# Graph attention on one Trainium2 core: edge rows gathered once per chunk of edges instead of once per step, steps addressed through a register

## The reference

```python
def _transformer_conv(x, src, dst, qw, qb, kw, kb, vw, vb, sw, sb):
    q = (x @ qw + qb).reshape(N, H, D); k = (x @ kw + kb).reshape(N, H, D); v = ...
    alpha = jnp.einsum('ehd,ehd->eh', q[dst], k[src]) * scale
    m = jax.ops.segment_max(alpha, dst, num_segments=N)
    ex = jnp.exp(alpha - m[dst])
    denom = jax.ops.segment_sum(ex, dst, num_segments=N)
    w = ex / (denom[dst] + 1e-16)
    agg = jax.ops.segment_sum(w[:, :, None] * v[src], dst, num_segments=N)
    return agg.mean(axis=1) + x @ sw + sb
h = _transformer_conv(x, src, dst, layer 1) + x @ lin1_w + lin1_b
out = _transformer_conv(h, src, dst, layer 2) + h @ lin2_w + lin2_b
return _layernorm(x + out, axis=-1)
```

## Time and profile before

| | |
|---|---|
| time, median of 3 runs | 1239.3 us (1238.72 to 1239.43) |
| profiled execution, span from first to last instruction | 1238.0 us, 30556 instructions |
| PE busy | 993.4 us (80%) |
| DVE busy | 983.5 us (79%) |
| ACT busy | 784.5 us (63%) |
| POOL busy | 801.5 us (65%), 832 gathers |
| mean granted TensorE clock | 0.940 |

### The profile page before, as it was taken

One profiled execution on the slowest core, in us unless ns is written; L12 is line 12 of the kernel. 1 busy time (PEld: TensorE's weight loads), 2 busy tenths in 40 slices (PEclk: granted clock), 3 DMA queues, 4 the chain that ended last, 5 costly groups with the idle time before them and its releaser, 6 DMA issues.

```text
span 1238.0 us, 30556 instructions
## 1 busy us (share of the span) xinstructions
PE 993.4 (80%) x6796; PEld 791.4 (64%) x6796; DVE 983.5 (79%) x5252; ACT 784.5 (63%) x2594; POOL 801.5 (65%) x854
## 2 busy tenths in 40 slices
PE   4868987878877878789896776978886878888887
PEld 2647766766666667678653655757675757667775
DVE  4799986878787878889567687878787887879876
ACT  0456866676676768677254564758575768678655
POOL 3777777777777777750057777777777777777100
PEclk9989999899999999999797999999899999999888
DMA  4223332222222222210032222222232323222001
GB/s 112 88 77 89 89 84 80 78 80 80 78 81 80 78 82 84 73 42 1 27 102 79 79 80 77 80 80 78 80 87 71 89 73 85 77 80 63 17 2 52
DMA packets 53531, 90.21 MB, mean 73 GB/s; under 512 B 17499, under 2 KB 25969, under 8 KB 53361
## 3 DMA queue, kind: packets, MB, share of 16 engines
q0 software_dynamic: 26624, 54.58, 16.4%
q1 hardware_dynamic: 24145, 32.62, 8.7%
q10 hardware_dynamic: 2592, 1.07, 0.3%
HBM read 84.86 MB, written 3.34 MB: 71 GB/s over the span
## 4 chain that ended last, share of the span: by engine, by line
DMA 28%; PE 21%; POOL 20%; issue 15%; DVE 13%; ACT 2%; DVEq 1%; SPq 0%; POOLq 0%; ACTq 0%
POOL gathered L407 20%; DMA gathered<-h_rows,src_e 14%; DMA gathered<-in_x,src_e 14%; PE ps L679 9%; PE ps L667 5%; DVE acc L961 4%; DVE junk L930 3%; PE ps L767 2%; PE ps L751 1%; PE ps L762 1%; ACT whot L508 1%; DVE max_b L999 1%; DVE apart L941 1%; DVE max_f L997 1%; PE ps L655 0%
## 5 line engine op out<-in xcount | busy, mean ns | idle before, releaser
L508 ACT ACTIVATE whot<-apart,below 128x128 f32<-128x128 bf16 x1664 | 550.3, 388 | 139.7 <-DVE apart L941 127.5
L679 PE MATMUL ps<-gathered,whot 128*128 128x129 f32 x3328 | 566.1, 297 | 62.4 <-ACT whot L508 44.0
L930 DVE SCALAR_TENSOR_TENSOR junk<-ps,gathered 128x129 f32<-128x129 f32 x1664 | 413.0, 286 | 163.6 <-issue 113.8
L667 PE MATMUL ps<-table,hot_t 128*128 x2496 | 445.7, 287 | 101.8 <-DVE junk L930 80.5
L679 PEld LDWEIGHTS ps<-gathered,whot 128*128 128x128 f32 x3328 | 457.1, 200 | 100.0 <-DVE acc L961 64.7
L407 POOL DMA_INDIRECT gathered<-in_x,src_e x416 | 399.8, 961 | 144.3 <-issue 68.0
L407 POOL DMA_INDIRECT gathered<-h_rows,src_e x416 | 397.5, 955 | 126.6 <-issue 62.2
L667 PEld LDWEIGHTS ps<-table,hot_t 128*128 128x128 bf16 x2496 | 249.3, 100 | 212.3 <-issue 157.3
L961 DVE TENSOR_TENSOR acc<-ps,acc 128x258 f32 x832 | 350.2, 421 | 14.9 <-PE ps L679 5.4
L492 ACT ACTIVATE apart<-col_b,ndl_e 128x128 bf16<-128x128 bf16 x618 | 239.2, 387 | 0.0
L930 DVE DVE_READ_ACCUMULATOR junk<-ps,gathered 128x1 f32 x1664 | 134.9, 81 | 0.4
(11 more groups left out here) (165 smaller groups left out, 561.0 us busy)
## 6 DMA issues: line engine op xcount, KB each, us to landing
dl_bc<-local_dst_rows SPq DMA_DIRECT2D x104, 256.0 KB
gathered<-in_x,src_e POOLq DMA_INDIRECT x416
gathered<-h_rows,src_e POOLq DMA_INDIRECT x416
h_rows<-table SPq DMA_DIRECT2D x6, 256.0 KB, 2.3
out<-x_rows SPq DMA_DIRECT2D x6, 256.0 KB
table<-in_L_gnn_q_w ACTq DMA_DIRECT2D x2, 128.0 KB
table<-in_L_gnn_k_w ACTq DMA_DIRECT2D x2, 128.0 KB
wv<-in_L_gnn_v_w ACTq DMA_DIRECT2D x2, 128.0 KB
```

What stands on the lines that cost most here:

```text
L508: last = nc.scalar.activation(whot[:, c % UN, h, :], apart[:, c % UN, :], ACT.Exp, scale=FAR, bias=below[:, j % 2, h, o:o + 1])
L667: last = nc.tensor.matmul(bank_t[n % NB][:, 0:CW], hot_t[:, n // BC % 2, t % BC, :], table[:, bass.ds(b, 1), part, :].rearrange("p o c -> ...
L679: last = nc.tensor.matmul(bank_u[n % NB][:, h * C1:(h + 1) * C1], whot[:, c % UN, h, :], gathered[:, c % RING, :], start=True, stop=True)
L930: last = V.scalar_tensor_tensor(out=junk[:, t % 2, h, :], in0=bank_t[n % NB][:, h * C1:(h + 1) * C1], scalar=1.0, in1=gathered[:, t % RING ...
```

## The change

POOL gathers each chunk once: 391 gathers a layer in place of 416, chunk c into slot c % 98. All steps of a chunk read that one slot. As the chunk of a step depends on the data, `step_alpha` on DVE and `step_u` on PE take the slot number from a register, loaded from a new list `slot_i`, and `bins_of` and `slots_of` now load eight steps at a time (RB = 8) where one list was loaded by four. `step_alpha(t)` still waits for gather t, and from step 391 on for none. A slot is free once all bins that its chunk can have are done, which is 24 steps later than before, so gather c waits for u step c - 74 where it waited for c - 98.

The indices no longer need `sel`: `src_e` is the transposed source list, 128 chunks from a first transpose, the rest from three more. SP loads the source list first, DVE converts it first, PE transposes it first, and DVE's other preparation stands behind that. `prepare(1)` has a 97th row for the slots, and a few small DVE instructions compute chunk modulo 98.

```diff
-                bin_i[0:1, step:step + UN], engines=[etype], min_val=0, max_val=BINS - 1,
+                bin_i[0:1, step:step + RB], engines=[etype], min_val=0, max_val=BINS - 1,
+        def slots_of(etype, step):
+            _, v = nc.values_load_multi_w_load_instructions(
+                slot_i[0:1, step:step + RB], engines=[etype], min_val=0, max_val=RING - 1,
...
+        def newest(t):
+            return min(t, CHUNKS - 1)
@@ sync
-            sp.wait_ge(S["pads_set"], 4)
-            for d, t in ((dst_d, dst_i), (src_d, src_i)):
+            for d, t, s, pads in ((src_d, src_i, S["src_in"], S["src_pad"]), (dst_d, dst_i, S["edges_in"], S["pads_set"])):
...
@@ gpsimd
-            pool.wait_ge(S["prep_copied"], 1)
-                for t in range(STEPS):
-                    n = l * STEPS + t
-                    if t >= RING:
-                        pool.wait_ge(S["u_ready"], n - RING + 1)
+                for c in range(CHUNKS):
+                    n = l * CHUNKS + c
+                    if l == 0 and c in (0, P):
+                        pool.wait_ge(S["prep_copied" if c else "src_e_ready"], 1)
+                    if c >= RING:
+                        pool.wait_ge(S["u_ready"], l * STEPS + c - RING + SPAN + 1)
...
-                        out=gathered[:, t % RING, 0:F], out_offset=None, in_=rows[:, :],
-                        in_offset=bass.IndirectOffsetOnAxis(ap=src_e[:, t:t + 1], axis=0),
+                        out=gathered[:, c % RING, 0:F], out_offset=None, in_=rows[:, :],
+                        in_offset=bass.IndirectOffsetOnAxis(ap=src_e[:, c:c + 1], axis=0),
@@ tensor
-            pe.wait_ge(S["sel_ready"], 1)
+            pe.wait_ge(S["ident_ready"], 1)
+            pe.wait_ge(S["src_ready"], 1)
+            nc.tensor.transpose(bank_t[0][:, 0:P], src_f[:, 0, :], ident[:, :]).then_inc(S["src_tp"], 1)
...
+                if r == 0:
+                    for t in range(1, CT):
+                        last = nc.tensor.transpose(b[:, t * P:(t + 1) * P], src_f[:, t, :], ident[:, :])
@@ step_u
-                                            gathered[:, c % RING, :], start=True, stop=True)
+                                            gathered[:, bass.ds(slot, 1), :].rearrange("p o c -> p (o c)"),
+                                            start=True, stop=True)
@@ vector
+            dve.wait_ge(S["src_in"], 16 * 3)
+            V.tensor_copy(src_f[:, 0, :], src_i[:, 0, :]).then_inc(S["src_ready"], 1)
+            V.tensor_copy(src_f[:, 1:CT, :], src_i[:, 1:CT, :]).then_inc(S["src_ready"], 1)
+            dve.wait_ge(S["src_tp"], 1)
+            V.tensor_copy(src_e[:, 0:P], bank_t[0][:, 0:P]).then_inc(S["src_e_ready"], 1)
...
+            V.tensor_copy(slot_i[:, :], bank_r[96:97, 0:STEPS])
@@ step_alpha
-                dve.wait_ge(got[n % GQ], 16 * (n // GQ + 1))
+                if t == newest(t):
+                    dve.wait_ge(got[m % GQ], 16 * (m // GQ + 1))
...
-                        in1=gathered[:, t % RING, :], op0=ALU.mult, op1=ALU.mult,
+                        in1=gathered[:, bass.ds(slot, 1), :].rearrange("p o c -> p (o c)"), op0=ALU.mult, op1=ALU.mult,
```

More of the change, by code:

```diff
@@ L40 @@
 UN = 4
+RB = 8
 BC = 8
@@ L62 @@
 BLOCK_OF = tuple(j for j in range(NBLK) for _ in range(SIZES[j]))
-assert CHUNKS + BINS - 1 <= STEPS and STEPS % BC == 0
+assert CHUNKS + BINS - 1 <= STEPS and STEPS % BC == 0 and STEPS % RB == 0
+SPAN = BINS - 1
+assert RING > SPAN + max(SIZES) + S_SLOTS + 1 and CHUNKS < 4 * RING
 assert LATE_ROWS + 2 * (ROW_SETS - 1) < LATE_DST and LATE_MASKS + T_AHEAD + 2 <= MASK_TILE
@@ L168, in program @@
         part128 = sb("part128", [P, 1])
-        src_e = sb("src_e", [P, STEPS], i32)
+        src_e = sb("src_e", [P, CT * P], i32)
+        ring_f = sb("ring_f", [P, 3, CT])
         ndl_e = sb("ndl_e", [P, STEPS])
         bin_i = sb("bin_i", [1, STEPS], i32)
+        slot_i = sb("slot_i", [1, STEPS], i32)
         link = sb("link", [2, STEPS + 1])
@@ L371, in _, with iota @@
         def _(pool):
+            def iota(t, step, n, base_step):
+                return nc.gpsimd.iota(t, [[step, n]], base=0, channel_multiplier=base_step,
+                                      allow_small_or_imprecise_dtypes=True)
+            nc.gpsimd.memset(src_i[:, CT - 1, :], 0).then_inc(S["src_pad"], 1)
+            iota(col_f[:, :], 1, P, 0)
+            iota(part_f[:, :], 0, 1, 1).then_inc(S["frame_set"], 1)
             nc.gpsimd.memset(dst_i[:, CT - 1, :], PAD_NODE).then_inc(S["pads_set"], 1)
-            nc.gpsimd.memset(src_i[:, CT - 1, :], 0).then_inc(S["pads_set"], 1)
             nc.gpsimd.memset(prev_i[:, 0:1], 0)
@@ L571, in prepare @@
                 b = banks[r % 2]
-                if r in (0, 1, PREP - 1):
-                    src = {0: src_f, 1: ends}.get(r, dst_f)
+                if r == 0:
+                    pe.wait_ge(S["src_ready"], 2)
+                    for t in range(1, CT):
+                        last = nc.tensor.transpose(b[:, t * P:(t + 1) * P], src_f[:, t, :], ident[:, :])
+                elif r in (1, PREP - 1):
+                    src = ends if r == 1 else dst_f
                     for t in range(CT):
@@ L786, in _, with copied @@
             step = chain(dve, S["dve_step"])
+            dve.wait_ge(S["frame_set"], 1)
+            V.tensor_scalar(ident[:, :], col_f[:, :], part_f[:, 0:1], None, ALU.is_equal).then_inc(S["ident_ready"], 1)
+            dve.wait_ge(S["src_in"], 16 * 3)
[3 more added lines that the diff above has]
+            V.tensor_copy(src_e[:, 0:P], bank_t[0][:, 0:P]).then_inc(S["src_e_ready"], 1)
+            def copied(r, ins):
+                ins.then_inc(S["prep_copied"], 1)
+            dve.wait_ge(S["prep_mm"], 1)
+            copied(0, V.tensor_copy(src_e[:, P:CT * P], bank_s[:, P:CT * P]))
             dve.wait_ge(S["consts_set"], 1)
@@ L804, in _ @@
             step(last)
+            for m in (2, 3):
+                last = V.scalar_tensor_tensor(out=ring_f[:, 2 - m % 2, :], in0=ring_f[:, 0, :], scalar=float(m * RING),
+                                              in1=ring_f[:, 1 + m % 2, :], op0=ALU.is_ge, op1=ALU.add)
+                step(last)
             for t in range(CT):
@@ L810, in _ @@
             V.tensor_copy(ends[:, :, 64], chunk_f[:, :])
+            V.scalar_tensor_tensor(out=ends[:, :, 96], in0=ring_f[:, 1, :], scalar=-float(RING), in1=ring_f[:, 0, :],
+                                   op0=ALU.mult, op1=ALU.add)
             for t in range(CT):
@@ L821, in _ @@
             V.memset(seg_b[:, :, 0:1], 0.0)
-            def copied(r, ins):
-                ins.then_inc(S["prep_copied"], 1)
-            dve.wait_ge(S["prep_mm"], 1)
-            copied(0, V.tensor_copy(src_e[:, :], bank_s[:, 0:STEPS]))
             dve.wait_ge(S["weights_in"], 16 * N_WEIGHT_DMA)
@@ L1041, in _ @@
                             one_hot_t(q0 + a // BC + 1)
-                        step_alpha(l, a)
+                        if a % RB == 0:
+                            slot = slots_of(DVE, a)
+                        step_alpha(l, a, slot[a % RB])
                     if s is not None:
```

53 lines of the change are left out of this document (28 added, 25 removed).

## The result

| | before | changed |
|---|---|---|
| time, median of 4 runs each, side by side | 1239.01 us | 1224.11 us (1223.71 to 1225.93) |
| ratio | | 0.9887 [0.9873, 0.9901] |
| profiled span | 1238.0 us | 1222.2 us |
| DVE, PE busy | 983.5, 993.4 us | 981.6, 998.6 us |
| POOL gathers | 832 | 782 |

14.9 us faster, against 20.3 forecast (1219.0, range 1212 to 1231). In the spans it is 15.8 us.

A forecast was written before the change was run, and what follows sets the result against it. POOL's gathers set the pace; DVE and PE bind the early stretch and the tails. The span was 1238.0 - 16.3 - 6.0 + 2.0 = 1217.7 us, with 1.3 around it 1219.0 us, range 1212 to 1231.

The forecast's parts named there:

- The start: Before layer 1: first gather at 5.7 us instead of 22.5, 16.8 gained, less 0.5 for crowding, so 16.3 us, all kept.
- The charge for crowding: Early gathers of layer 1: thirteen more run beside DVE's preparation, 0.04 us charged each, 0.5 us in all, bound 1.1.
- Twenty-five freed steps: Score steps behind 390, no gather left to wait for: 3.0 us gained a layer, 6.0 in all, bounds 0 and 3.7 a layer.
- Register instructions: Slot registers on DVE and PE: 0 in the score steps, +1.0 us in each layer's tail (u steps behind the scores).
- The bound of 0.14 on DVE: Score steps: at worst, nothing hidden and a load doubling with its values, register work adds 0.14 us a step on DVE.
- the 0.12 from which the start would have been lost: Score steps: from 0.12 us a step of added cost, the start's gain begins to go.
- The ring: Gathers waiting for u steps to free slots: cost 0, bound 2 us; 11 steps to spare before gather 169.
- (c): Rival: a register load grows with its number of values, 0.69 us for eight, +0.086 us a step: 1229 us, chance 0.05.
- (b): Rival: register work is exposed on DVE by 0.14 us a step, 7 us gained of 16: 1238 us, chance 0.07.
- (d): Rival: all 25 removed gathers pay, 63 us, and the start 16: 1160 us, chance 0.03.
- (e): Rival: slower, as a register-addressed score step costs DVE 0.20 us or more: 1262 us, slower from about 0.15, chance 0.06.
- The port: Gathers beside DVE's preparation: DVE's 2-port modes lock GpSimd out of its descriptor port, which could shrink the start's gain.

The follow-up runs named there:

- e3: Changed kernel with the slot of score and u steps written into the program instead of taken from registers: 1217.79 us, ratio 0.9843 to the kernel before.
- e4: Changed kernel with score steps waiting for the gather of the chunk they read, by constants from this input: 1178.93 us, ratio 0.9529 to the kernel before.
- e2: Changed kernel with POOL's first gather held until prepare(1) is copied, about as late as before: 1238.80 us, ratio 1.0016 to the kernel before.
- group 2: Follow-up runs on another chip, kernel before at 1623.78 us; the changed kernel run there again unchanged took 1633.89 us, ratio 1.0064.

## Why the prediction was right, and where it was off

**The start, -16.3.** Right in mechanism and size: 16.6 at the first gather. The charge for crowding, 0.5 us, is what is gone by gather 208 (16.6 to 16.1). Another 1.5 us go between gathers 208 and 390, where the prediction had nothing, and no run shows why (e3 and e4, with the same gathers, lose 0.8 and 0.4 there against before). The scores were said to catch up near step 160 and did near 195, since the 78 steps that are set side by side under e3 took 0.08 us each more than before. From step 104 to 195 they took 1.065 us a step, where 1.05 was worked out. The step stands because that left room under 1.26. e2 shows that this term is all of the gain.

**Twenty-five freed steps, -6.0.** This failed. From gather 390 issued to the last score it is 35.6 us before and 35.5 after (551.9 - 516.3, 537.2 - 501.7), and 35.4 against 35.3 in layer 2: 0.2 in all. Score 390 comes 7.6 us behind its gather instead of 6.0, and the 25 steps behind it take 27.9 instead of 29.6. The step took 96.5% fill for granted, and DVE has 24.04 / 27.9 = 86%. In e3 the 25 steps take 25.3 us (DVE 95% busy) and the way from gather 390 is 34.1: half of the 3.0 us a layer is there when the register work is away, the other half is lost ahead of these steps, since score 390 came 8.8 us behind its gather there. Why it comes later than before in both kernels no run shows.

**Register instructions, 0 and +1.0 a tail.** The step "adds have had such an instruction all along, DVE's sequencer works ahead and I take 0" failed, and it is the mis-sized term: 5.4 us by e3. What I take to have been missed is that the sequencer's own time adds up; e3 shows the price, not this working of it. Per step, DVE's had 0.057 for the add and 0.343 / 4 of loading, 0.14 us; now it has 2 x 0.057 and 2 x 0.596 / 8, 0.26 us. My reading, which no run tests by itself, is that it works ahead while the engine is full and falls behind at each pair of loads, 1.2 us of sequencer time. The bound of 0.14 on DVE was close for an addition of 0.12; what was exposed is 0.06 to 0.08. That is under the 0.12 from which the start would have been lost, so it delayed the catching up, took half of what the freed steps could give, and left the start's gain. The tails took 0.2 and 0.7 us more, close to the 1.0 each; in the first the granted clock was 1.00 against 0.91 and PE was busy 33.12 us against 34.90, which may have hidden some of it.

**The ring, 0.** Right in size on this chip, but by luck. The prediction looked at gather 169, where 8.3 us were left; the tightest place is gather 134, where nothing was left and 0.17 us were lost with the next. It took 23 or more slots of lead as allowed at steps 100 to 130. The list of `slots()`, written out again, allows 22 at step 100, 19 at 116 to 127 and 18 at 130, and the lead was 19 at gather 134. Slower score steps would have made it bind in earnest: in group 2, where the steps are slower, POOL waits 414.5 us for PE.

**Not in the sum.** The two projections and the end gave 1.2 and 1.3 us, with no cause looked for; layer 2's gathers took 0.5 back. Around the span of the profiled execution lie 1.8 us (1224.0 against 1222.2), not 1.3. Together: -16.6 + 2.0 - 0.2 + 0.9 - 2.5 + 0.5 = -15.9, against the 15.8 of the spans.

**The rivals.** (c), the load that grows with its values, is true in its mechanism: 0.59 us for eight, not 0.34, or 0.063 us a step of the 0.086 that it took for certain. I gave it 0.05 because of nothing but the wish for one duration per instruction. (b), exposure on DVE by 0.14, was half true. They were priced at 1229 and 1238. The time came out 5.1 us above the forecast, where e3 puts 5.4 on the register work. (d) took 63 us for impossible since "the code excludes" that steps stop waiting in order. For this change that was right; e4 shows 45 us behind that order. (e) would have needed 0.15 a step. The rule behind it (Trainium skill, Runtime: NRT & Kernel Launch, "Instruction fetch mechanics", about 200 ns for each register) does not hold for these lists: 65 ns a value. But its direction, that bulk does not make it free, is what my sum lacked.

**The port.** The prediction named the Trainium skill (SBUF — State Buffer, "Who interferes with whom"). The gathers at 13.59 and 15.26 us above took 1.36 and 1.66 us. The first ran wholly beside DVE's compares with two SBUF inputs (L856), the second beside their last 0.6 us and the casts and memsets behind them:

```profile
11.69 1.48 DVE L848 TENSOR_SCALAR acc<-acc,key 128x416 f32<-128x416 f32 x4
...
13.50 2.33 DVE L856 SCALAR_TENSOR_TENSOR acc<-acc,keyprev 128x416 f32<-128x416 f32 x4
```

The gather beside L848, with one tensor input, took 1.04. The section says of instructions with two SBUF inputs that they hinder a GpSimd instruction that reads SBUF. A gather reads its indices there, so the first of the two agrees with that, though whether it is this port no run here shows. The prediction took the gather of 1.87 us for a sign of the 2-port modes. Beside it the kernel before ran compares with two SBUF inputs:

```profile
56.65 1.47 DVE L878 TENSOR_TENSOR table<-table 48x1270 bf16<-48x1270 f32 x1
57.07 1.87 POOL L407 DMA_INDIRECT gathered<-in_x,src_e  x1 [0.30 <-issue]
...
58.05 1.48 DVE L879 TENSOR_TENSOR in_last<-table 48x1280 bf16<-48x1280 f32 x1
```

So it goes rather with what the section says on two inputs, as the gather beside L856 does.

## What to carry to other kernels

Work that is taken from the engine that sets the pace pays only if its consumers stop waiting in the old order: of 25 gathers fewer a layer nothing came on the first chip until the score steps waited for the chunk they read, and then 45 us. Count a sequencer's time like an engine's: loads by their number of values, one operation for each operand that a register addresses, and ask in which stretch the engine is too full to hide it. An early start of the pacing engine is kept, here 14.5 of 16.6 us, if the consumers have room per step to catch up and the ring is deep enough for the lead until they have. Look for the tightest place of the ring, not for one place.

## What the runs showed that was not expected

- A load into registers takes about 73 ns and 65 ns for each value (332, 591, 1106 ns for 4, 8, 16): longer lists save little.
- An indirect gather whose 128 rows are all the same one took 743 ns a packet against 132, with the DMA engines 88% busy at 40 GB/s.
- On two of three chips the same kernels took 31 to 33% longer, with PE idle up to 64.5 us at a time for "issue" at the start of a layer, and at their usual pace once the gathers of a layer had ended. There the changed kernel is 0.3 to 0.6% slower than before, not 1.1% faster. Why is open.
